# Where the normalised context rows are kept, and what ScalarE waits for before it writes them

## The chip, the cores and the metric

The kernel runs on one core of a Trainium2 chip. A core has five engines, each with its own queue of instructions in a fixed order: TensorE (PE in the profile; its weight loads are PEld), VectorE (DVE), ScalarE (ACT), GpSimd (POOL) and SyncE (SP, which starts the DMAs here). They meet only at semaphores. The metric is the time of one execution on the device in microseconds, median of the runs; lower is better.

## The reference

`x` is (128, 64, 128): 128 batch elements of 64 tokens and 128 features. `ctx_1024` (the context) has the same shape, `cond_1024` is (128, 128). Four layers follow each other:

```
L0: x += gate * selfattn(mod(ln(x)));  x += crossattn(ln(x), context);      x += gate * mlp(mod(ln(x)))
L1: x += crossattn(mod(ln(x)), mod(ln(context)))
L2: x += gate * selfattn(mod(ln(x)));  x += crossattn(ln(x), ln(context));  x += gate * mlp(mod(ln(x)))
L3: x += gate * mixture_of_3_experts(ln(x), evidence from context)
```

All attentions have 16 heads of 8 features. `ln` normalises the 128 features of a token. The context is normalised twice for each batch element, once in L1 and once in L2. The result of `ln(context)` depends on the input alone, and not on `x`.

## The kernel before

Work is cut into 32 groups of 4 batch elements (256 tokens). Six streams (`STREAMS`) each take every sixth group; a stream has its own set of tiles, and its next group starts when the one before is done. A group passes through `GROUP_STEPS`, some 75 steps such as `stats`, `normal`, `cols` (a layer norm and the transposition of its result), `q`, `k`, `v`, `tops`, `lows`, `scores`, `values`, `out` (an attention), `fc1`, `fc2` (an MLP). The order in which the steps of the six streams follow each other is a table, `SEQUENCE`, and it is the same on all engines: every engine walks `ORDER` from first to last and issues its own part of each step. So an instruction that waits holds up everything behind it on its engine, whatever stream that belongs to. In the middle of the table the pattern repeats: a stretch of some 343 us comes again and again.

PSUM has eight banks, in two halves of four. `tops` and `scores` take one half, and all other results of TensorE take the banks of the other half in turn. `bank_plan` fixes from the tables which bank each result takes, and who must have emptied it (`HELD_BEFORE`).

The steps that matter here, for a cross attention whose context is normalised:

- `stats` (VectorE, L1034 and L1037): mean and variance of the rows of `x`. In the same step ScalarE computes the normalised context rows, `cn_rows = c_rows * c_rstd + c_minus` (L1175, two instructions, one per half of 256 tokens). The scale and the offset were computed by GpSimd when the group began. This happens 64 times (32 groups, L1 and L2).
- `kvnorm` (TensorE, L802): `cn_rows` is transposed into PSUM, and ScalarE (L2) or VectorE (L1) moves it into `kvT`, from which keys and values are made.
- `normal` (VectorE, L1043) writes `n_rows`; `cols` (TensorE L802, then ScalarE L1163 or VectorE L1049 and L1050) turns them into `nT`, the normalised columns of x, for `q` or `fc1`.
- `lows`: TensorE turns the maxima of the scores (L870), and ScalarE moves them negated into `low` (L1163), a view of the tile `o_rows`. `scores` then uses `low` as a weight (L881), adds the scores (L885), and ScalarE takes the exponentials (L1212).
- `out` and `fc2`: VectorE adds the residual into `x_rows` (L1015 where it is gated, L1089 where not).

`cn_rows` is a view of the tile `o_rows`. That tile also holds `low` and, after `values`, the weighed rows that VectorE turns (L1079, L1082) before `out`. L1175 therefore waits, beside `c_scaled` (the scale is there), for `x_changed(n)`, that is, for the last residual sum of the same stream, which comes from the step `fc2` of L0 or from `out` of L2's self attention.

Of the kernel before, what the change touches and what calls it, by code (L numbers as in the profile page):

```python
# [257 lines left out]
def used_by(n, ring, back=0):  # L258

    s = ORDER[n][2]  # L260
    while back:
        n -= 1
        back -= ORDER[n][2] == s
    return int(USED[n][ring])


def residual_before(n):


    s, last, gated = ORDER[n][2], None, 0  # L270
    for m in range(n):
        kind, arg, t = ORDER[m]
        if t == s and kind == "load":
            last = None
        if t == s and kind in ("out", "fc2", "l3_out"):
            last = m
            gated += kind == "l3_out" or arg["gate"] is not None
    return last, gated


def round_of(n):

    return sum(kind == "load" and s == ORDER[n][2] for kind, _, s in ORDER[:n + 1]) - 1
# [80 lines left out]
def build(nc, x, cond, context, weights, biases, rows, ident_in, own_head_in, own_ones_in, gate_store, out):  # L364
# [3 lines left out]
    with ExitStack() as ctx:  # L368
# [3 lines left out]
        def each(name, shape, dt=F32):  # L372
            return [sb(f"{name}{i}", shape, dt) for i in range(STREAMS)]
# [23 lines left out]
        nT, kvT = each("nT", [D, GROUP, SEQ]), each("kvT", [D, GROUP, SEQ])  # L397
# [13 lines left out]
        o_rows = each("o_rows", [D, TOK])  # L411
        inv_sum = each("inv_sum", [D, GROUP * 4, 2])
        low = [o[:, 0:D] for o in o_rows]
        cn_rows = [o[:, :].rearrange("p (t c) -> p t c", t=2) for o in o_rows]
        weighed = [q[:, :, :, :].rearrange("p g l q -> p (g l q)") for q in q_heads]
        oT = kvT

# [107 lines left out]
        def x_changed(n):  # L525

            last, gated = residual_before(n)
            s = ORDER[n][2]
            if last is None:
                return x_in[s], 16 * (round_of(n) + 1)  # L530
            if ORDER[last][0] == "out" and ORDER[last][1]["gate"] is None:
                return v_emptied, used_by(last, FOR_VECTOR)
            return x_added[s], gated
# [12 lines left out]
        with nc.Block() as block:  # L546
# [37 lines left out]
            def _(pe):  # L584
# [7 lines left out]
                for n, (products, _) in enumerate(product_banks):  # L592
                    pe.wait_ge(turned_in, 3)
                    at = 0
                    for lhsT, rhs in products:
                        mm = nc.tensor.matmul(bank[7 if n == 0 else 3 + n][:, at:at + rhs.shape[1]], lhsT, rhs, start=True, stop=True)
                        at += rhs.shape[1]
                    mm.then_inc(products_filled, 1)
                pe.wait_ge(cond_moved, 2)
                for n in range(M_COND):  # L600
                    if n >= 4:
                        pe.wait_ge(mods_moved, n - 3)
                    dst = bank[n % 4][:, 0:B]
                    if n < M_EXPERT:
                        name, _, block_, _, _, _ = MODS[n]
                        mm = nc.tensor.matmul(dst, w(name, 0, block_), cond_silu[:, :], start=True, stop=True)
                    elif n < M_GATE:
                        e, r = divmod(n - M_EXPERT, 2)
                        mm = nc.tensor.matmul(dst, w("L3_e_w1", 3 * e + 2, 2 * 0 + r), mods[:, M_COND, :], start=True, stop=True)
                    else:  # L610
                        mm = nc.tensor.matmul(dst, w("L3_gate_w1", 2), mods[:, M_COND, :], start=True, stop=True)
                    mm.then_inc(mods_filled, 1)
# [10 lines left out]
                for n, (name, block_, _) in enumerate(GATES):  # L623
                    mm = nc.tensor.matmul(bank[6][0:B, n * D:(n + 1) * D], cond_silu[:, :], w(name, 0, block_), start=True, stop=True)
# [60 lines left out]
        with nc.Block() as block:  # L685
# [472 lines left out]
            def _(act):  # L1158
# [6 lines left out]
                for n, (kind, arg, s) in enumerate(ORDER):  # L1165
# [3 lines left out]
                    if kind == "stats" and n in CONTEXT_NORMS:  # L1169

                        e = CONTEXT_NORMS[n]
                        act.wait_ge(c_scaled[s], round_of(n) + 1)
                        act.wait_ge(*x_changed(n))
                        for t in range(2):
                            m = nc.scalar.activation(cn_rows[s][:, t, :], c_rows[s][:, t, :], ACT.Identity,  # L1175
                                                     scale=c_rstd[s][:, e, t:t + 1], bias=c_minus[s][:, e, t:t + 1])
                        m.then_inc(c_normed[s], 1)
# [123 lines left out]
```

## Time and profile before

| | us |
|---|---|
| median of 3 runs | 1933.61 (1929.34 to 1938.17) |
| time of the profiled execution | 1929.33 |
| its span, first to last instruction | 1927.5 |
| busy: PE, DVE, ACT, POOL | 1781.7, 1640.5, 1384.0, 643.6 |
| granted TensorE clock, mean share of full speed | 0.982 |

TensorE is busy for 92% of the span and VectorE for 85%. Matmul ends are modelled, so a busy TensorE isn't TensorE at its peak. The profiled execution took 1.8 us more than its span, and 4.3 us less than the median of the three runs. DMAs play no part after the start: the 16 DMA engines are busy below 10% from the third fortieth of the span on.

### The profile page before, as it was taken

Reading aid. Unit: us, or ns where it says so; the run is one execution under the profiler, and the core shown is the slowest. Engines: PE = TensorE matmul, PEld = TensorE weight load, DVE = VectorE, ACT = ScalarE, POOL = GpSimd, SP = SyncE. Lnnn points to the kernel's source line nnn. Section 1 sums busy time; section 2 is a strip of 40 time slices with the busy share of each in tenths; the row PEclk is TensorE's granted clock in tenths of the full one; section 3 lists DMA queues with packets and bytes.
Section 4 is the critical chain, followed back from the end, with each engine's and each line's share of the span. In section 5 each row is a group of like instructions: output and inputs, shape, how many; then the busy total and the mean of one; then the engine's idle time right before and its main releaser. Section 6 shows DMA issues by size and latency. Waiting matters only on the chain.

```text
span 1927.5 us, 88160 instructions
## 1 busy us (share of the span) xinstructions
PE 1781.7 (92%) x38181; PEld 1523.1 (79%) x38181; DVE 1640.5 (85%) x4236; ACT 1384.0 (72%) x3340; POOL 643.6 (33%) x1145
## 2 busy tenths in 40 slices
PE   3787999999999999999999999999999988989898
PEld 3666778888777888887878888787888877877788
DVE  2887889899988899997889999888999977988874
ACT  1554677787767778876777787777777776767697
POOL 1431324333323333442233333333333332332241
PEclk9999999999999999999999999999999999999999
DMA  4200000000000000000000000000000000000000
GB/s 164 61 13 9 17 17 14 17 22 22 22 22 9 16 23 22 22 23 22 3 22 22 23 22 22 22 3 22 22 22 23 22 9 18 20 14 9 9 5 15
DMA packets 57166, 42.62 MB, mean 22 GB/s; under 512 B 13520, under 2 KB 55632, under 8 KB 56528
## 3 DMA queue, kind: packets, MB, share of 16 engines
q1 hardware_dynamic: 56784, 36.99, 6.4%
q8 instruction: 306, 5.01, 1.0%
q14 instruction: 76, 0.62, 0.1%
HBM read 32.51 MB, written 4.46 MB: 19 GB/s over the span
## 4 chain that ended last, share of the span: by engine, by line
PE 66%; DVE 21%; ACT 7%; issue 3%; DMA 0%; POOL 0%; SPq 0%; ACTq 0%; DVEq 0%; POOLq 0%
PE half L981 9%; PE half L881 8%; PE half L861 7%; PE half L885 7%; PE half L900 6%; DVE top L1070 6%; PE half L928 4%; PE half L918 4%; PE half L802 4%; PE half L990 3%; PE half L848 3%; PE half L911 3%; PE half L837 3%; PE half L833 3%; ACT pT L1247 2%
## 5 line engine op out<-in xcount | busy, mean ns | idle before, releaser
L1070 DVE TENSOR_REDUCE top<-half 128x32 f32<-128x2048 f32 x160 | 365.0, 2282 | 63.0 <-PE half L861 61.9
L761 POOL TENSOR_TENSOR shifted<-moments,eps 128x2 f32<-128x2 f32 x256 | 50.6, 198 | 1091.0 <-DVE moments L1037 1090.9
L1212 ACT ACTIVATE pT<-half 128x512 f32<-128x512 f32 x640 | 327.9, 611 | 117.2 <-PE half L885 116.4
L881 PE MATMUL half<-o_rows,of_keys 32*128 32x128 f32 x5120 | 283.6, 290 | 16.3 <-ACT o_rows L1163 14.3
L885 PE MATMUL half<-q_heads,k_heads 32*128 32x128 f32 x5120 | 270.4, 279 | 1.6 <-issue 1.6
L881 PEld LDWEIGHTS half<-o_rows,of_keys 32*128 32x128 f32 x5120 | 214.9, 194 | 38.8 <-ACT o_rows L1163 20.3
L1247 ACT ACTIVATE pT<-half,mod 128x64 f32<-128x64 f32 x896 | 195.9, 334 | 48.5 <-PE half L981 47.3
L885 PEld LDWEIGHTS half<-q_heads,k_heads 32*128 32x128 f32 x5120 | 217.1, 196 | 2.8 <-issue 2.5
L861 PE MATMUL half<-k_heads,q_heads 32*128 32x128 f32 x5120 | 191.4, 285 | 9.9 <-issue 5.3
L1192 ACT ACTIVATE k_heads<-half,key_bias,own_head_sb 128x256 f32<-128x256 f32 x320 | 163.2, 570 | 46.3 <-PE half L837 45.0
L861 PEld LDWEIGHTS half<-k_heads,q_heads 32*128 32x128 f32 x5120 | 163.8, 191 | 37.7 <-issue 23.2
L1043 DVE TENSOR_SCALAR n_rows<-x_rows,moments,rstd 128x128 f32<-128x128 f32 x512 | 189.3, 416 | 3.9 <-POOL rstd L763 3.0
L763 POOL TENSOR_TENSOR rstd<-shifted,minus_halves 128x2 f32<-128x2 f32 x256 | 185.3, 724 | 20.1
L900 PEld LDWEIGHTS half<-pT,v_cols 128*32 128x32 f32 x10240 | 152.2, 110 | 38.1 <-issue 29.1
L900 PE MATMUL half<-pT,v_cols 128*32 128x64 f32 x10240 | 175.5, 220 | 6.7 <-ACT pT L1212 5.1
L1062 DVE TENSOR_SCALAR q_heads<-half,b_sb,own_head_sb 128x256 f32<-128x256 f32 x320 | 156.4, 532 | 11.9 <-PE half L833 11.7
L981 PE MATMUL half<-nT,w_sb 128*128 128x256 f32 x448 | 137.9, 390 | 0.0
L918 PE MATMUL half<-nT,w_sb 128*128 128x256 f32 x512 | 135.6, 393 | 1.0 <-DVE nT L1050 0.8
L1200 ACT ACTIVATE v_cols<-half 64x256 f32<-64x256 f32 x320 | 122.6, 383 | 18.6 <-PE half L848 16.5
L981 PE MATMUL half<-pT,w_sb 128*128 128x256 f32 x448 | 133.7, 380 | 0.0
L1217 ACT ACTIVATE pT<-half,b_sb 128x256 f32<-128x256 f32 x256 | 106.1, 471 | 35.6 <-PE half L918 34.4
L928 PE MATMUL half<-w_sb,pT 128*128 128x128 f32 x1024 | 127.3, 278 | 0.1
(151 smaller groups left out, 3747.3 us busy)
## 6 DMA issues: line engine op xcount, KB each, us to landing
gates<-gate_store SPq DMA_DIRECT2D x128, 128.0 KB, 3.0
x_rows<-x SPq DMA_DIRECT2D x32, 128.0 KB, 2.1
c_rows<-context SPq DMA_DIRECT2D x32, 128.0 KB, 2.7
out<-x_rows SPq DMA_DIRECT2D x32, 128.0 KB, 1.8
w_sb<-weights SPq DMA_DIRECT2D x1, 2368.0 KB, 12.7
pT<-weights SPq DMA_DIRECT2D x1, 1024.0 KB, 4.8
logit_bias<-logit_store SPq DMA_DIRECT2D x64, 1.5 KB, 3.5
row_sb<-rows SPq DMA_DIRECT2D x1, 769.5 KB, 6.3
```

The costliest lines, as they stand in the source:

```text
L763: nc.gpsimd.tensor_tensor(rstd[s][:, :], shifted[s][:, :], minus_halves[:, 0, :], ALU.pow).then_inc(rstd_in[s], 1)
L861: mm = nc.tensor.matmul(halves[HALF_OF[n]][:, g, tb * D:(tb + 1) * D], q_heads[s][part, tb, :, :], k_heads[s][part, tb, :, :], start=True, ...
L881: nc.tensor.matmul(halves[HALF_OF[n]][:, g, tb * D:(tb + 1) * D], of_keys[part, 2 * tb:2 * tb + 2, :], low[s][part, :], start=True, stop=F ...
L885: mm = nc.tensor.matmul(halves[HALF_OF[n]][:, g, tb * D:(tb + 1) * D], k_heads[s][part, tb, :, :], q_heads[s][part, tb, :, :], start=False ...
L900: mm = nc.tensor.matmul(dst[QUAD * g:QUAD * (g + 1), tb, :, lo, :], v_cols[s][:, at:at + QUAD], pT[s][:, g, tb, lo, :].rearrange("p (h q) ...
L918: mm = nc.tensor.matmul(dst[:, c * TOK:(c + 1) * TOK], w(layer["w1"], 0, 2 * half + c), nT[s][:, :, :], start=True, stop=True)
L928: mm = nc.tensor.matmul(dst[:, t * D:(t + 1) * D], hidden[s][:, c, t * D:(t + 1) * D], w(arg["w2"], c), start=c == 0, stop=c == 3)
L981: mm = nc.tensor.matmul(dst[:, r * TOK:(r + 1) * TOK], weight, src[:, :, :], start=c == 0, stop=c == 1)
L1043: m = nc.vector.tensor_scalar(n_rows[s][:, t, :], x_rows[s][:, t, :], moments[s][:, t, 0:1], rstd[s][:, t:t + 1], ALU.subtract, ALU.mult)
L1070: nc.vector.tensor_reduce(top[s][:, :].rearrange("p (g c) -> p g c", c=32)[:, :, 0:2 * GROUP], halves[HALF_OF[n]][:, :, :].rearrange("p g ...
L1212: nc.scalar.activation(turn_cols[s][:, g, :], halves[HALF_OF[n]][:, g, :], ACT.Exp, scale=ATT_SCALE).then_inc(scores_read, 1)
L1247: m = nc.scalar.activation(dst, src[:, at], ACT.Silu, bias=mod[s][:, k, tb:tb + 1])
```

## The change

The normalised context rows become a view of `nT` instead of one of `o_rows`, with the same shape (128 x 2 x 128), and ScalarE's wait for the residual sum is taken out. The rest of the program stands as it was.

```
-        cn_rows = [o[:, :].rearrange("p (t c) -> p t c", t=2) for o in o_rows]
+        cn_rows = [c[:, :, :].rearrange("p (t b) q -> p t (b q)", t=2) for c in nT]
...
                         e = CONTEXT_NORMS[n]
                         act.wait_ge(c_scaled[s], round_of(n) + 1)
-                        act.wait_ge(*x_changed(n))
                         for t in range(2):
                             m = nc.scalar.activation(cn_rows[s][:, t, :], c_rows[s][:, t, :], ACT.Identity,
                                                      scale=c_rstd[s][:, e, t:t + 1], bias=c_minus[s][:, e, t:t + 1])
```

After the first hunk `nT` has two uses: ScalarE writes the context rows into it at `stats`, TensorE reads them at `kvnorm`, and then `cols` of the same norm writes the columns of x over them. On ScalarE the line moves from L1175 to L1174, and those below it move up by one as well.

No instruction changes its place on any engine. This is the queue of ScalarE at one of the 64 places, in the stretch around 537 us of the trace, before:

```order
L1163 ACTIVATE o_rows2<-half0 128x128 [waits a_filled]
L1175 ACTIVATE o_rows1<-c_rows1,c_minus1,c_rstd1 128x128 [waits x_added1,c_scaled1]
L1175 ACTIVATE o_rows1<-c_rows1,c_minus1,c_rstd1 128x128
L1163 ACTIVATE kvT1<-half0 128x256 [waits a_filled]
L1163 ACTIVATE o_rows4<-half0 128x128 [waits a_filled]
L1212 ACT_TABLE_LOAD
L1212 ACTIVATE pT2<-half1 128x512 [waits scores_filled] x4
```

and of the change:

```order
L1163 ACTIVATE o_rows2<-half0 128x128 [waits a_filled]
L1174 ACTIVATE nT1<-c_rows1,c_minus1,c_rstd1 128x128 [waits c_scaled1]
L1174 ACTIVATE nT1<-c_rows1,c_minus1,c_rstd1 128x128
L1163 ACTIVATE kvT1<-half0 128x256 [waits a_filled]
L1163 ACTIVATE o_rows4<-half0 128x128 [waits a_filled]
L1211 ACT_TABLE_LOAD
L1211 ACTIVATE pT2<-half1 128x512 [waits scores_filled] x4
```

The number behind a tile is its stream. The output tile is another one and the semaphore `x_added1` is gone; the neighbours are the same.

## Rows read from the trace of the kernel before

**Rows 1.** The page: busy time by engine, and the shares of the chain.

```profile
PE 1781.7 (92%) x38181; PEld 1523.1 (79%) x38181; DVE 1640.5 (85%) x4236; ACT 1384.0 (72%) x3340; POOL 643.6 (33%) x1145
PE 66%; DVE 21%; ACT 7%; issue 3%; DMA 0%; POOL 0%; SPq 0%; ACTq 0%; DVEq 0%; POOLq 0%
```

**Rows 2.** L1175 alone: ScalarE's idle time before it; who waited for it (us, times).

```profile
  DVE x_rows L1015: 65.3, 31
  PE half L802: 27.0, 17
```

**Rows 3.** Timeline at 533 to 545 us: start, duration, engine, line, [idle before <-releaser].

```profile
532.91 0.28 ACT L1163 ACTIVATE o_rows<-half 128x128 f32<-128x128 f32 x1 [0.53 <-PE half L870]
...
534.49 0.61 PE L911 MATMUL half<-w_sb,kvT 128*128 128x128 f32 x4
...
537.30 0.88 ACT L1175 ACTIVATE o_rows<-c_rows,c_minus,c_rstd 128x128 f32<-128x128 f32 x2 [4.12 <-DVE x_rows L1015]
...
538.23 0.44 PE L802 MATMUL half<-ident_sb,o_rows 128*128 128x128 f32 x2 [3.13 <-ACT o_rows L1175]
...
544.60 0.43 DVE L1049 TENSOR_TENSOR half<-half,mod 128x256 f32<-128x256 f32 x1 [5.54 <-PE half L802]
```

**Rows 4.** Timeline two rounds of the pattern later, at 1223 to 1228 us.

```profile
1222.93 0.44 PE L802 MATMUL half<-ident_sb,o_rows 128*128 128x128 f32 x2 [3.13 <-ACT o_rows L1175]
...
1227.67 0.43 DVE L1049 TENSOR_TENSOR half<-half,mod 128x256 f32<-128x256 f32 x1 [3.92 <-PE half L802]
```

**Rows 5.** Timeline at 588 to 600 us.

```profile
588.27 1.57 ACT L1217 ACTIVATE pT<-half,b_sb 128x256 f32<-128x256 f32 x4
...
590.64 0.65 PE L848 MATMUL half<-w_sb,nT 128*32 128x64 f32 x32
...
593.08 0.88 ACT L1175 ACTIVATE o_rows<-c_rows,c_minus,c_rstd 128x128 f32<-128x128 f32 x2 [3.25 <-DVE x_rows L1015]
...
594.17 0.81 PE L881 MATMUL half<-o_rows,of_keys 32*128 32x128 f32 x8 [2.88 <-ACT o_rows L1163]
...
599.75 2.29 DVE L1070 TENSOR_REDUCE top<-half 128x32 f32<-128x2048 f32 x1 [5.96 <-PE half L861]
```

**Rows 6.** Timeline at 118 to 122 us: the same two instructions elsewhere.

```profile
118.76 0.50 PE L881 MATMUL half<-o_rows,of_keys 32*128 32x128 f32 x8 [0.37 <-ACT o_rows L1163]
...
121.93 2.29 DVE L1070 TENSOR_REDUCE top<-half 128x32 f32<-128x2048 f32 x1 [0.16 <-PE half L861]
```

**Rows 7.** Timeline at 244 to 258 us: VectorE's restart there.

```profile
256.14 2.29 DVE L1070 TENSOR_REDUCE top<-half 128x32 f32<-128x2048 f32 x1 [5.04 <-PE half L861]
```

**Rows 8.** Timeline at 154 to 165 us.

```profile
154.15 2.25 DVE L1070 TENSOR_REDUCE top<-half 128x32 f32<-128x2048 f32 x1
...
158.22 0.69 PE L802 MATMUL half<-ident_sb,o_rows 128*128 128x128 f32 x2 [3.23 <-ACT o_rows L1175]
...
164.93 2.29 DVE L1070 TENSOR_REDUCE top<-half 128x32 f32<-128x2048 f32 x1 [6.28 <-PE half L861]
```

**Rows 9.** Timeline at 1619 to 1622 us.

```profile
1619.00 0.44 PE L802 MATMUL half<-ident_sb,o_rows 128*128 128x128 f32 x2 [1.03 <-ACT o_rows L1175]
...
1621.33 1.19 PE L998 MATMUL half<-w_sb,pT 128*128 128x128 f32 x4 [1.89 <-ACT pT L1247]
```

**Rows 10.** Timeline at 282 to 285 us.

```profile
282.08 0.44 PE L802 MATMUL half<-ident_sb,o_rows 128*128 128x128 f32 x2 [1.14 <-ACT o_rows L1175]
...
284.27 2.29 DVE L1070 TENSOR_REDUCE top<-half 128x32 f32<-128x2048 f32 x1 [0.82 <-PE half L861]
```

**Rows 11.** Timeline, two more waits of TensorE for L1175.

```profile
109.00 0.44 PE L802 MATMUL half<-ident_sb,o_rows 128*128 128x128 f32 x2 [1.77 <-ACT o_rows L1175]
...
1708.31 0.44 PE L802 MATMUL half<-ident_sb,o_rows 128*128 128x128 f32 x2 [1.28 <-ACT o_rows L1175]
```

**Rows 12.** Windows: start:end, length, busy time of PE, PEld, DVE, ACT, POOL, PEclk, DMA share, GB/s.

```profile
538.71:542.13 3.42, 3.42 (x65) 3.42 (x68) 0.31 (x3) 1.83 (x3) 1.55 (x3) 0.53 0.02 5
...
908.00:910.00 2.00, 2.00 (x47) 2.00 (x42) 1.70 (x10) 0.21 (x1) 0.51 (x2) 0.50 0.63 179
```

More of the change, by code:

```diff
@@ L413, in build @@
         low = [o[:, 0:D] for o in o_rows]
-        cn_rows = [o[:, :].rearrange("p (t c) -> p t c", t=2) for o in o_rows]
+        cn_rows = [c[:, :, :].rearrange("p (t b) q -> p t (b q)", t=2) for c in nT]
         weighed = [q[:, :, :, :].rearrange("p g l q -> p (g l q)") for q in q_heads]
@@ L1172, in _ @@
                         act.wait_ge(c_scaled[s], round_of(n) + 1)
-                        act.wait_ge(*x_changed(n))
                         for t in range(2):
```

## The prediction, made before the change was run

> **What bounds the kernel now.** I began with the page. TensorE is busy for 92% of the span and VectorE for 85%, and the chain of work that ended last runs over TensorE for 66%, over VectorE for 21% and over ScalarE for 7% [rows 1]. So the pace is TensorE's, with stretches in which it waits for a result that came through VectorE, and ScalarE matters only where it is the messenger. ScalarE is such a messenger at the line that the change touches. The view of L1175 alone says that ScalarE stood idle before it for 65.3 us, in 31 of the 64 places, and that the last thing to come was always the residual sum of VectorE (L1015); TensorE in turn stood idle for 27.0 us, 17 times, because the context rows came late [rows 2]. All of TensorE's idle time is 1927.5 - 1781.7 = 145.8 us, so this one wait ends nearly a fifth of it. The other views are timelines around those places, read for two questions: when would ScalarE have been free, and what does VectorE wait for next. The second decides whether a gain lasts: every engine walks the same table, so a place gives its full gain when TensorE arrives earlier at a point where VectorE stood idle waiting for it for at least as long.
>
> **What the change costs.** Nothing is added. The two instructions at each place have the same input and the same shape, and write another tile of SBUF; I take 0.88 us per pair as before [rows 3]. A price of the other tile can't be read from the trace; since the same input and 128 output partitions are moved, I put it at nothing. The new home adds no wait: the last readers of `nT` before the place are TensorE's products for `fc1`, or for `q`, `k` and `v`, and ScalarE has itself already emptied the products, or taken the exponentials that depend on them. Behind it `cols` writes `nT` only after TensorE's transpositions, which come after `kvnorm` in its queue. The wait for the scale stays; GpSimd wrote it at the start of the group, tens of microseconds earlier.
>
> **What the removed wait gives, place by place.**
>
> *A, four places (the one at 537 us and its repetitions near 879, 1222 and 1565).* ScalarE is free at 532.91 + 0.28 = 533.19 and waits 4.12 us. TensorE ends `out` at 534.49 + 0.61 = 535.10 and waits 3.13 us for the rows [rows 3]. By the tables, the bank of this `kvnorm` was last held by a product of `fc1` that ScalarE has emptied, so VectorE doesn't hold it. Without the wait the rows are there at 533.19 + 0.88 = 534.07, and `kvnorm` starts at 535.10. From there to VectorE's restart (L1049) it took 544.60 - 538.23 = 6.37 us here, but 1227.67 - 1222.93 = 4.74 us two rounds later, over the same instructions [rows 3, 4]. The difference, 1.63 us, is TensorE's clock: it was granted 0.53 of full speed, that is the 1.2 GHz level nearly throughout, right after the gap at 538 [rows 12], and the full 2.4 GHz in the round at 1223. So VectorE restarts at 535.10 + 4.74 = 539.84 instead of 544.60: 4.76 us. VectorE is free from 544.60 - 5.54 = 539.06 on, so it doesn't stand in the way. Three of the four rounds are of this kind and one has no slow clock and gives 3.13 us: 3 x 4.76 + 3.13 = 17.4 us.
>
> *B, four places (near 250, 593, 937 and 1278).* TensorE doesn't wait for L1175 itself but for `low`, which stands behind it on ScalarE: 2.88 us at 594.17. ScalarE would be free at 588.27 + 1.57 = 589.84, done with the context rows at 590.72 and with `low` at about 591.0, and TensorE ends L848 at 590.64 + 0.65 = 591.29 [rows 5]. L881 starts then. From L881 to the restart of VectorE (L1070) it takes 121.93 - 118.76 = 3.17 us at full clock [rows 6], so VectorE restarts at 594.46 instead of 599.75: 5.29 us. It is free from 599.75 - 5.96 = 593.79 on. At the other three places VectorE's idle time is 0.92 us shorter, 5.04 instead of 5.96 (one stands in [rows 7]), since less of the way was at half clock; 5.29 - 0.92 = 4.4 us each. Sum 5.3 + 13.1 = 18.4 us.
>
> *157 us.* TensorE waits 3.23 us for L1175, but then needs the half of PSUM from which VectorE takes maxima until 154.15 + 2.25 = 156.40. `scores` starts at about 156.5, VectorE restarts at 159.7 instead of 164.93 [rows 6, 8]: 5.2 us.
>
> *1619 us.* TensorE waits 1.03 us for L1175 and 1.89 us for the expert activations behind it on ScalarE [rows 9]; with the slow clock that follows (1.63 as in A) 4.6 us.
>
> *C, four places (near 281, 625, 967, 1308).* TensorE waits 1.14 us, but VectorE idles only 0.82 us at its next wait for TensorE [rows 10]. I take 0.9 each: 3.6 us.
>
> *The rest.* At 109 us TensorE waits 1.77 us; at 1708 it is 1.28 us and a stretch at half clock follows, 2.9 with it [rows 11]. 1.8 + 2.9 = 4.7 us. Of the 27.0 us of [rows 2] these places hold 12.5 (A) + 3.2 + 1.0 + 4.6 (C) + 1.8 + 1.3 = 24.4. The other 2.6 us are small waits, mostly in a stretch that comes some 24 us behind C in each round, where VectorE works without a pause and TensorE stops for it again soon after; I put them at nothing, 2.6 us at most. What ScalarE waited beyond all this held up nobody that the trace shows.
>
> The sum is 17.4 + 18.4 + 5.2 + 4.6 + 3.6 + 4.7 = 53.9 us. Of it some 38 are idle time of TensorE and 16 are half clock (4.9 in A; 1.48 three times and 2.4 once in B; 1.2 to 1.7 at 157, 1619 and 1708).
>
> **The clock.** TensorE also fell to half speed where it had not stood still for long: at 908 to 910 us the granted clock is 0.50 [rows 12], and TensorE had gone from one product to the next before it with only short stops. There are three such stretches in the trace, none of which this wait explains, and each cost about what A shows, 1.63 us. So a part of the clock's 16 us may come back at other places. I allow for three new ones, 5 us, and forecast 53.9 - 5 = 49 us.
>
> The Trainium skill's page "TensorE: Matmul & The Clock Gate" has a rule for either side. Its section "HAM oscillation — how this bites in real kernels" says that a wait between bursts of matmuls lets the clock fall and the next burst starts slow; by that all 16 us come back and the gain is 54 us. The trace agrees at 538 and disagrees at 1223, where the same gap of 3.13 us was followed by full clock. The section "A second HAM failure mode: psum-queue depth-cycling" says that frequent small idle gaps between groups of matmuls are enough for the clock to swing, which speaks against counting the clock at all; the stretch at 908 agrees. That is the second rival below.
>
> The profiled execution took 1929.33 us; less 49 is 1880. The median of the runs shown lies 4.3 us higher, so the forecast is **1884 us**, 2.6% below 1933.61.
>
> **The rivals.**
>
> *VectorE takes the pace* (chance 0.17). It is busy for 85% of the span and in the steady part for more. What TensorE gains at the places above is drawn from idle time that VectorE then no longer has, and if other waits of TensorE for VectorE grow in return, only part stays. Against it: at each large place VectorE's own idle time is longer than the gain. Half of the gain would stay: 1933.6 - 27 = 1906 us.
>
> *The clock doesn't come back* (0.14). TensorE falls to half speed as often as before, at other gaps. For it: the three stretches without a long gap. Only the 38 us of idle time are won: 1896 us.
>
> *It doesn't do what it says* (0.06). The context rows are early, but TensorE finds the next obstacle at the same place, a bank that VectorE has still to empty, or the maxima that it has still to take, as at 157 [rows 8]. Against it: at A the bank is ScalarE's, and at B L881 was held by `low`, which only ScalarE had still to write [rows 5]. Then the gain is what is left at 109 and C, some 0 to 5 us: 1931 us.
>
> *Slower* (0.03). TensorE, now stopping in many small steps and not in a few long ones, drops to half clock more often. A stretch costs 1.63 us. With all 53.9 - 16 = 38 us of idle time won, it takes more than 23 new stretches before the kernel is slower, against 13 or so now; with 30 of them it is 1945 us. Only if the idle time is not won either does a handful suffice.
>
> **How the numbers follow.** The forecast has 0.60, and its own range is 1872 (all of the sum, 54 us, and 8 us for what I put at nothing: the 2.6 us above, and places where ScalarE waited and something other than L1175 was late in consequence) to 1896. The range for 8 in 10 reaches up to most of the first rival: 1868 to 1908. What a measurement of this kernel can tell from no change is about 0.5%, 9.7 us. The forecast and the first two rivals are faster by more, and a sliver of the third: 0.92. Same: 0.05. Slower: 0.03.
>
> **What would show it.** In the profile of the changed kernel the line of the context rows (L1174) has no idle time that VectorE's residual sum ends, and no wait of TensorE for it above 0.5 us. VectorE's idle time of 5.54 and 5.96 us at the restarts of A and B [rows 3, 5] falls below 1 us. TensorE's busy time falls too, by about as much as the half clock gives back, and the mean granted clock rises from 0.982 to about 0.99. The repeating stretch shrinks from 343 us to about 333. The prediction is wrong if the gaps of 3 us at A and B are still there under another releaser, or gone while the repeating stretch keeps its length; and the sum is wrong in its clock term if the idle time goes but the granted clock stays at 0.98.

## The result, and the profile after

| kernel | median us | lowest to highest | runs |
|---|---|---|---|
| before | 1931.47 | 1928.68 to 1938.17 | 4 |
| after | 1868.8 | 1866.06 to 1869.83 | 4 |

The changed kernel takes 0.9668 of the time, with a 95% interval of 0.9639 to 0.9698: some 63 us less, where 49 were forecast. The profiled execution took 1866.06 us, its span is 1864.3 us and its mean granted clock 0.996. The time lies 15 us under the forecast of 1884. That is 3 us below the low end of the forecast's own range (1872), and just inside the range for 8 in 10 (1868 to 1908).

Lines of the page of the changed kernel: busy time by engine, TensorE's granted clock in 40 slices of the span, the chain that ended last, and VectorE's maxima (busy us, mean ns, idle time ahead of them). The last line is the same row before.

```profile
PE 1756.0 (94%) x38181; PEld 1502.5 (81%) x38181; DVE 1639.4 (88%) x4236; ACT 1383.1 (74%) x3340; POOL 643.9 (35%) x1145
...
PEclk9899999999999999999999999999999999999999
...
PE 74%; DVE 14%; ACT 6%; issue 3%; DMA 0%; POOL 0%; SPq 0%; DVEq 0%; POOLq 0%
...
L1070 DVE TENSOR_REDUCE top<-half 128x32 f32<-128x2048 f32 x160 | 365.1, 2282 | 29.4 <-PE half L861 27.8
...
L1070 DVE TENSOR_REDUCE top<-half 128x32 f32<-128x2048 f32 x160 | 365.0, 2282 | 63.0 <-PE half L861 61.9
```

Against [rows 1] the number of matmuls is unchanged and TensorE is busy for 25.7 us less; its idle time is 1864.3 - 1756.0 = 108.3 us, where it was 145.8. That is 37.5 us less idle time and 25.7 us less busy time for the same work, together the 63.2 us by which the span is shorter. VectorE's share of the chain fell from 21% to 14%. It is busy for as long as before and only waits less: ahead of its maxima 29.4 us, where it was 63.0.

The view of the line of the context rows in the changed kernel (durations in ns, then who idled before it and who for it):

```profile
L1174 ACT ACTIVATE nT<-c_rows,c_minus,c_rstd x128: 478/487/554, 105.8 to 1774.7; 128x128 f32<-128x128 f32 x128
its engine sat idle before it (us, times) until:
who waited for it (us, times):
  PEld half L802: 0.2, 1
```

Both numbers of [rows 2] are gone: nothing stands under "sat idle before it", where there were 65.3 us, and TensorE's 27.0 us have shrunk to a single 0.2 us.

The timeline of the changed kernel at the first of the four places A, which answers to [rows 3]:

```profile
519.80 0.28 ACT L1163 ACTIVATE o_rows<-half 128x128 f32<-128x128 f32 x1 [0.52 <-PE half L870]
519.98 0.87 ACT L1174 ACTIVATE nT<-c_rows,c_minus,c_rstd 128x128 f32<-128x128 f32 x2
...
521.39 0.61 PE L911 MATMUL half<-w_sb,kvT 128*128 128x128 f32 x4
...
521.84 0.38 PE L802 MATMUL half<-ident_sb,nT 128*128 128x128 f32 x2
...
526.51 0.43 DVE L1049 TENSOR_TENSOR half<-half,mod 128x256 f32<-128x256 f32 x1 [0.57 <-PE half L802]
```

ScalarE goes from the copy straight to the context rows, TensorE goes from `out` straight to `kvnorm`, and VectorE waits 0.57 us where it waited 5.54. From `kvnorm` to VectorE's restart it is 526.51 - 521.84 = 4.67 us; I had reckoned with the 4.74 of [rows 4].

The same at the second of the four places B, which answers to [rows 5]:

```profile
570.17 1.57 ACT L1216 ACTIVATE pT<-half,b_sb 128x256 f32<-128x256 f32 x4
...
571.61 0.89 ACT L1174 ACTIVATE nT<-c_rows,c_minus,c_rstd 128x128 f32<-128x128 f32 x2
...
572.54 0.65 PE L848 MATMUL half<-w_sb,nT 128*32 128x64 f32 x32
...
573.12 0.50 PE L881 MATMUL half<-o_rows,of_keys 32*128 32x128 f32 x8
...
576.15 2.29 DVE L1070 TENSOR_REDUCE top<-half 128x32 f32<-128x2048 f32 x1 [0.44 <-PE half L861]
```

L881 has no idle time before it any more (2.88 us before), and VectorE waits 0.44 us (5.96 before). Windows of five microseconds around the place A show full clock (the columns are those of [rows 12]):

```profile
520.00:525.00 5.00, 5.00 (x117) 4.83 (x120) 4.90 (x13) 3.34 (x8) 1.20 (x2) 1.00 0.02 5
525.00:530.00 5.00, 5.00 (x210) 4.43 (x207) 4.15 (x16) 4.99 (x12) 1.74 (x4) 1.00 0.02 5
```

**Where the 63 us came from, place by place.** VectorE takes its maxima (L1070) 160 times, in the same order in both kernels. If the start of each is subtracted from the start of its counterpart before, the difference is a staircase, and each step is what one place gave:

| place (time in the kernel before) | forecast | step measured |
|---|---|---|
| 109 us | 1.8 | 2.0 |
| 157 us | 5.2 | 5.4 |
| A, four places | 17.4 | 4.97, 4.44, 3.34, 4.98: 17.7 |
| B, four places | 18.4 | 4.57, 5.52, 4.05, 4.39: 18.5 |
| C, four places | 3.6 | 0.87, 1.19, 1.19, 1.37: 4.6 |
| 1619 us | 4.6 | 5.46 and 1.36: 6.8 |
| 1708 us | 2.9 | 3.5 |
| the small waits some 24 us behind C, four places | 0 | 0.91 each: 3.6 |
| stretches at half clock near 225, 908 and 1248 us | -5 (the old three stay, three new ones) | 2.15, 1.63, 1.63: 5.4, the old ones gone |
| all other steps, up and down, 1.8 at most | 0 | -4.2 |
| sum | 48.9 | 63.3 |

### The profile page after: what moved, and what is told of

Its sections match the earlier page's. It is cut to its first block, busy times and chain, and to the rows that moved or that the text cites. A ratio compares the mean times of both kernels' runs of the same rounds, so it can differ in the third digit from the quotient of the medians.

```text
span 1864.3 us, 88096 instructions
## 1 busy us (share of the span) xinstructions
PE 1756.0 (94%) x38181; PEld 1502.5 (81%) x38181; DVE 1639.4 (88%) x4236; ACT 1383.1 (74%) x3340; POOL 643.9 (35%) x1145
## 4 chain that ended last, share of the span: by engine, by line
PE 74%; DVE 14%; ACT 6%; issue 3%; DMA 0%; POOL 0%; SPq 0%; DVEq 0%; POOLq 0%
PE half L981 9%; PE half L881 8%; PE half L861 7%; PE half L900 7%; PE half L885 7%; PE half L928 5%; PE half L918 5%; DVE top L1070 4%; PE half L802 4%; PE half L990 4%; PE half L848 4%; PE half L911 3%; PE half L833 3%; PE half L837 3%; ACT pT L1246 2%
## 5 line engine op out<-in xcount | busy, mean ns | idle before, releaser
L1070 DVE TENSOR_REDUCE top<-half 128x32 f32<-128x2048 f32 x160 | 365.1, 2282 | 29.4 <-PE half L861 27.8
L881 PE MATMUL half<-o_rows,of_keys 32*128 32x128 f32 x5120 | 273.8, 281 | 5.1 <-ACT o_rows L1163 3.0
L885 PE MATMUL half<-q_heads,k_heads 32*128 32x128 f32 x5120 | 261.4, 271 | 3.0 <-issue 2.9
L881 PEld LDWEIGHTS half<-o_rows,of_keys 32*128 32x128 f32 x5120 | 205.9, 186 | 26.3 <-issue 11.5
L885 PEld LDWEIGHTS half<-q_heads,k_heads 32*128 32x128 f32 x5120 | 207.8, 187 | 5.4 <-issue 5.4
L861 PEld LDWEIGHTS half<-k_heads,q_heads 32*128 32x128 f32 x5120 | 160.0, 186 | 37.3 <-issue 21.6
L1062 DVE TENSOR_SCALAR q_heads<-half,b_sb,own_head_sb 128x256 f32<-128x256 f32 x320 | 156.6, 533 | 10.4 <-PE half L833 10.0
## 6 DMA issues: line engine op xcount, KB each, us to landing
w_sb<-weights SPq DMA_DIRECT2D x1, 2368.0 KB, 12.7
```

What stands on the lines that cost most here:

```text
L861: mm = nc.tensor.matmul(halves[HALF_OF[n]][:, g, tb * D:(tb + 1) * D], q_heads[s][part, tb, :, :], k_heads[s][part, tb, :, :], start=True, ...
L881: nc.tensor.matmul(halves[HALF_OF[n]][:, g, tb * D:(tb + 1) * D], of_keys[part, 2 * tb:2 * tb + 2, :], low[s][part, :], start=True, stop=F ...
L885: mm = nc.tensor.matmul(halves[HALF_OF[n]][:, g, tb * D:(tb + 1) * D], k_heads[s][part, tb, :, :], q_heads[s][part, tb, :, :], start=False ...
L1070: nc.vector.tensor_reduce(top[s][:, :].rearrange("p (g c) -> p g c", c=32)[:, :, 0:2 * GROUP], halves[HALF_OF[n]][:, :, :].rearrange("p g ...
```

## The experiments

**Home only: the new tile with the old wait.** Does the tile matter, or only the wait?

```
                         e = CONTEXT_NORMS[n]
                         act.wait_ge(c_scaled[s], round_of(n) + 1)
+                        act.wait_ge(*x_changed(n))      # the rest as in the changed kernel
```

> The context rows live in nT as in the change, but ScalarE's wait for the residual sum is put back. Theory (the wait is everything): ratio to the kernel before 1.000 within 0.3%, 65 us of idle time before the line again. Rival (the other tile itself saves or costs something): a ratio away from 1 by more than 0.3%, up to the whole 0.967.

Measured: 1932.28 us (1925.04 to 1942.49, 10 runs), ratio 1.0 (0.998 to 1.002) to the kernel before. The view of its line, with the wait back:

```profile
L1175 ACT ACTIVATE nT<-c_rows,c_minus,c_rstd x128: 477/492/553, 109.5 to 1838.8; 128x128 f32<-128x128 f32 x128
its engine sat idle before it (us, times) until:
  DVE x_rows L1015: 65.2, 31
...
  PE half L802: 26.8, 17
```

The rows land in `nT` and everything is as before: 65.2 us in 31 places, 26.8 us in 17. The new home costs nothing and gives nothing; all of the gain is the wait's.

**One kind of norm keeps the wait.** Half of the 64 context norms, those of the kind LOOSE (all of them in L1), keep it; then the other half, of the kind TIGHT (all in L2).

```
+                        if CONTEXT_NORMS[n] == LOOSE:   # the other run: == TIGHT
+                            act.wait_ge(*x_changed(n))
```

> The change, with the wait kept for the 32 context norms of L1 (whose residual sum comes from fc2) and gone for the 32 of L2. By place: A, B, 157 and 1619 us belong to L2, so 17 + 18 + 5 + 5 = 46 us of the 54 of the sum are won, plus what the clock gives beyond it: about 1876 to 1882. Rival (the gain is spread over all waits of ScalarE, in proportion to its idle time): about half of 63 us, 1900.

> The mirror image: the wait gone for L1 and kept for L2. By place only C, 109 and 1708 us are won, 3.6 + 4.7 = 8 us: 1923. Rival (spread): 1900.

Measured: with LOOSE waiting 1877.08 us (1874.20 to 1879.79), ratio 0.9719 (0.9694 to 0.9745); with TIGHT waiting 1919.5 us (1916.68 to 1925.49), ratio 0.9942 (0.9919 to 0.9965). Against the 1931.84 us of the kernel before in the same set of runs, 54.8 us are won without the wait of the TIGHT norms, to which all places A and B belong, and 12.3 us without that of the LOOSE ones. The first time lies in the range expected (1876 to 1882), though 9 us more were won than the 46 of the places; the second is 3.5 us under the 1923 expected. The two gains sum to 67, not to 63, so the split holds to a few microseconds.

**The wait placed behind the rows.** Is it enough to have the rows early, or must the wait go?

```
-                        act.wait_ge(*x_changed(n))      # ahead of the two activations
                         ... (the two activations)
+                        act.wait_ge(*x_changed(n))      # behind them
```

> The change, with the wait for the residual sum put behind the two instructions instead of in front of them. The context rows are then early, but what stands behind them on ScalarE is as late as before. Theory (A and C are rows that come late, B and 1619 are the queue behind them): A, C, 109 and 157 stay won, B and 1619 are lost, 23 us and their clock: about 1892 to 1900. Rival (it is the queue behind the line that matters everywhere): nearly the time of before, 1925 or more. Rival (only the rows matter): 1870.

Measured: 1903.59 us (1899.50 to 1904.83), ratio 0.985 (0.9821 to 0.9878). Only 28 of the 63 us are won, fewer than the 32 to 40 expected. The timeline of this kernel at the place B shows why:

```profile
582.71 0.89 ACT L1174 ACTIVATE nT<-c_rows,c_minus,c_rstd 128x128 f32<-128x128 f32 x2
...
586.00 0.28 ACT L1163 ACTIVATE o_rows<-half 128x128 f32<-128x128 f32 x1 [2.40 <-DVE x_rows L1015]
...
586.33 0.50 PE L881 MATMUL half<-o_rows,of_keys 32*128 32x128 f32 x8 [2.04 <-ACT o_rows L1163]
...
590.69 2.29 DVE L1070 TENSOR_REDUCE top<-half 128x32 f32<-128x2048 f32 x1 [3.92 <-PE half L861]
```

The rows themselves are early, but ScalarE now stands at the wait with the copy for `low` behind it, and TensorE needs that copy: 2.04 us of its 2.88 are back. At A the copy of the transposed rows (into `kvT`) stands behind the wait in the same way. Both are in this kernel's list of waits (total us, times, longest):

```profile
ACT kvT L1163 <- DVE x_rows L1015: 16.7, 5, 3.5
...
ACT o_rows L1163 <- DVE x_rows L1015: 12.5, 5, 2.6
```

The expectation was wrong on this point: it had A and 157 us as wholly won. Measured as in the table above (starts of the maxima, here against the changed kernel), this kernel loses 1.6 to 1.7 us at each place A and 4.6 us at 157, beside 2.1, 3.5, 1.6 and 1.9 at B. The wait's price is not only in what it guards but in all that is queued behind it.

**The wait kept at the four places A, or at the four places B.** What is one gap worth, clock included?

```
+                        if n in (738, 1284, 1830, 2376):    # A; the other run: (276, 822, 1368, 1914), B
+                            act.wait_ge(*x_changed(n))
```

> The change, with the wait put back at the four places A alone (context norms of L2 near 537, 879, 1222 and 1565 us). Theory (the places add up and the clock falls because of these gaps): 4 x 3.13 = 12.5 us of idle time come back and half clock of 1.6 to 1.8 us behind most of them: 17 to 20 us above the change, 1886 to 1889. Rival (the clock falls by chance, wherever TensorE is at the time, and stays away in a faster kernel): 12.5 us, 1881.

> The change, with the wait put back at the four places B alone (near 250, 593, 937 and 1278 us). Theory: 4 x 2.9 = 11.6 us of idle time and 1.5 to 2.4 us of half clock behind each: 18 to 20 us above the change, 1887 to 1889. Rival (clock by chance): 1880.

Measured: A 1891.62 us (1889.67 to 1894.49), ratio 0.9801 (0.9776 to 0.9826), that is 22.8 us over the changed kernel; B 1884.57 us (1878.38 to 1888.69), ratio 0.9758 (0.9722 to 0.9794), 15.8 us over it. The timeline of the kernel with the wait at A, first place:

```profile
524.99 0.69 PE L802 MATMUL half<-ident_sb,nT 128*128 128x128 f32 x2 [3.13 <-ACT nT L1176]
...
532.44 0.43 DVE L1049 TENSOR_TENSOR half<-half,mod 128x256 f32<-128x256 f32 x1 [6.64 <-PE half L802]
```

and its windows around that place:

```profile
520.00:525.00 5.00, 1.86 (x18) 1.68 (x16) 4.86 (x14) 0.88 (x2) 1.20 (x2) 0.90 0.00 2
525.00:530.00 5.00, 5.00 (x79) 4.67 (x83) 0.77 (x6) 2.20 (x4) 1.74 (x4) 0.50 0.01 3
530.00:535.00 5.00, 5.00 (x196) 4.55 (x192) 2.38 (x8) 4.64 (x11) 0.00 (x0) 0.92 0.01 2
```

The idle time of 3.13 us is that of [rows 3] to the hundredth, but the way to VectorE's restart is 532.44 - 524.99 = 7.45 us, where the kernel before had 6.37 with one stretch at half clock and 4.74 with none. The clock of 0.90, 0.50 and 0.92 in three windows of 5 us takes 0.5 + 2.5 + 0.4 = 3.4 us, two stretches of 1.7 in a row. Behind all four gaps of this kernel the clock fell, twice for 3.4 and twice for 1.7 us. So the wait at A cost more than the 17 to 20 us expected and the one at B less than the 18 to 20; behind the four gaps of B the clock fell twice only. Times of different sets of runs carry some uncertainty of their own: the median of the kernel before was 1929.8 us beside these two and 1931.5 to 1932.0 beside the others, so 22.8 and 15.8 may be 2 to 3 us too low.

**The gaps kept, and filled.** This is the run that separates idle time from clock in the kernel before: TensorE still waits for the rows, but multiplies meanwhile. Six products of the identity with a weight tile go into the PSUM slot that the next transposition overwrites.

```
                     if kind == "kvnorm":
+                        slot = (to_v if isinstance(arg[1], tuple) else to_a).slot()
+                        if n in (151, 739, 1285, 1831, 2377):
+                            keep_busy(slot)             # 6 matmuls, results overwritten
                         count.next(c_normed[s])
...
                     if kind == "scores":
+                        wait_emptied(pe, HELD_BEFORE[n], emptied)
+                        if n in (279, 825, 1371, 1917):
+                            keep_busy(halves[HALF_OF[n]][:, 0, :])
                         after("low", s)
-                        wait_emptied(pe, HELD_BEFORE[n], emptied)
```

The products stand behind the wait for the slot and ahead of the wait for the data; for that the order of the two waits is turned round at every `kvnorm` and every `scores`. The trace records each product as two instructions, so six are 12.

> The kernel before, with the wait where it was, but at the four places A, the four places B and at 157 us TensorE fills its gap with six products (identity by weights, 2.6 us) whose result is overwritten. They change no output. Theory (the gaps make the clock fall): the idle time stays on the path, the half clock goes: 9 places at 1.5 to 2.4 us, 13 to 16 us faster than before, 1916 to 1919. Rival (the clock falls for another reason than standing still): no change, 1932, or slower where the fillers run over the end of a gap.

Measured: 1913.82 us (1910.61 to 1914.65), ratio 0.9912 (0.9887 to 0.9937), 16 us less than the kernel before, with more work and the same waits. The timeline and one window of this kernel at the first place A:

```profile
530.07 0.44 PE L802 MATMUL half<-ident_sb,o_rows 128*128 128x128 f32 x2 [0.54 <-ACT o_rows L1184]
...
534.81 0.43 DVE L1058 TENSOR_TENSOR half<-half,mod 128x256 f32<-128x256 f32 x1 [3.92 <-PE half L802]
```

```profile
530.00:535.00 5.00, 4.93 (x137) 4.64 (x138) 1.05 (x7) 4.22 (x9) 1.74 (x4) 1.00 0.02 5
```

534.81 - 530.07 = 4.74 us and clock 1.00: exactly the way of [rows 4]. In this profile the clock fell behind none of the nine filled gaps, where it had fallen behind eight of the nine before. Only what TensorE does while it waits was changed, so the 16 us are its clock. Not all of them need come from the nine places: the old stretches near 228, 908 and 1248 are gone as well, and a new one stands near 558.

**The gaps A kept and filled, in the changed kernel.** The same edit on the kernel that keeps the wait at A, n in (739, 1285, 1831, 2377), without the part for `scores`.

> The change, with the wait put back at the four places A, and six products (identity by weights, 2.6 us, overwritten afterwards, no output changes) in front of the context rows' transposition there. The version without the products took 1891.6 us, 22.8 more than the change. Theory (a gap of 3.13 us costs itself and the half clock that follows): 12.5 us stay, the rest goes: 1881. Rival (A costs more than its gap because something else is late there, not the clock): 1889 or more.

Measured: 1881.06 us (1880.43 to 1881.83), ratio 0.9739 (0.972 to 0.9759). Its timeline, first place A:

```profile
521.82 2.75 PE L807 MATMUL half<-w_sb,ident_sb 128*128 128x256 f32 x12
...
525.12 0.44 PE L802 MATMUL half<-ident_sb,nT 128*128 128x128 f32 x2 [0.54 <-ACT nT L1183]
...
529.85 0.43 DVE L1056 TENSOR_TENSOR half<-half,mod 128x256 f32<-128x256 f32 x1 [3.92 <-PE half L802]
```

TensorE is busy for 2.75 us of the gap, stops for 0.54, and the way behind it is 4.73 us instead of 7.45. Of the 22.8 us that the four gaps A cost, 10.5 were clock (1891.62 - 1881.06) and 12.3 are the wait itself, 3.1 each: the 3.13 us of the rows, four times. The two times are of different sets of runs; each against its own kernel before, the clock's part is 12.7 us. In the profiles the places A of this kernel lose 3.4 us three times and 4.5 once against the changed kernel, so the split is good to some 2 us and not to a tenth.

**The change once more, and with a busy start.** The second adds eight products while TensorE waits for the first DMAs, so that its clock is up when the work begins.

```
+                keep_busy(bank[7], 4)                   # ahead of the loop over ORDER
...
                     if kind == "cols":
+                        if n == FIRST_COLS:
+                            keep_busy(bank[7], 4)
```

> The change itself, again. Its time is 1867 to 1870. Asked is how much time the clock takes from it from run to run: the kernel before had mean clocks of 0.978 to 0.986 in its runs. If unexplained falls of the clock are chance and about as many as before (three to six a run), the mean clock lies at 0.990 to 0.993; if they go with the gaps, at 0.995 or above (0.996 is what is lost in the first 60 us alone).

> The change, with eight products (identity by weights, into a bank that isn't in use; no output changes) while TensorE waits for the first rows: four before the first transposition and four before the second. From 44 to 59 us the clock is at half in the change, and the work done in it is some 5 us. Theory: with TensorE kept busy, the clock is full when that work begins, and 2 to 3 us are saved: 1866. Rival (the wait for the rows hides the slow clock, or the products delay the first steps): 1869 or more. The difference is at the edge of what can be told.

Measured, on one chip: the change 1868.3 us (1867.05 to 1872.89), ratio 0.9678 (0.9656 to 0.9699); with the busy start 1863.46 us (1860.65 to 1866.51), ratio 0.9648 (0.9627 to 0.967). The windows of the start, first the changed kernel:

```profile
54.00:56.00 2.00, 1.54 (x4) 1.27 (x5) 1.23 (x5) 0.00 (x0) 1.50 (x3) 0.50 0.41 128
56.00:58.00 2.00, 2.00 (x37) 1.30 (x36) 1.54 (x6) 1.29 (x3) 1.69 (x4) 0.50 0.56 70
```

and the one with the busy start:

```profile
54.00:56.00 2.00, 1.98 (x40) 1.40 (x39) 1.72 (x6) 1.08 (x3) 0.84 (x4) 1.00 0.36 108
56.00:58.00 2.00, 2.00 (x38) 1.69 (x36) 1.76 (x6) 0.86 (x3) 1.84 (x4) 1.00 0.65 101
```

The same first products run at the 2.4 GHz level (clock 1.00) instead of the 1.2 GHz level (0.50), and the median is 4.8 us lower. This version beats both kernels. But the start does not account for the 4.8 us. In the two profiles VectorE's first maxima begin 2.3 us earlier with the busy start (57.32 against 59.59 us), as expected, and by 78 us the lead is gone (78.26 against 77.97), for with the busy start the clock fell at 69 us. The 4.4 us between the two spans build up later; the largest steps, 3.6 and 3.3 us, are where the profile of the repeated change has two stretches at half clock (222 and 502 us) and this one has none. That the products of the start prevent those is not shown.

The repeated change answers its own question. Its four executions had mean clocks of 0.994, 0.994, 0.992 and 0.990. One lies within what I had put down for falls by chance, as many as before (0.990 to 0.993), one at its low end, two just above it, and none at the 0.995 or above that falls by the removed gaps alone would give. So the changed kernel still loses its clock now and then. These windows of the profiled one,

```profile
220.00:225.00 5.00, 3.34 (x34) 2.84 (x34) 3.27 (x5) 0.93 (x4) 0.00 (x0) 0.73 0.02 3
...
500.00:505.00 5.00, 3.48 (x23) 2.61 (x19) 4.93 (x8) 1.29 (x4) 2.36 (x3) 0.72 0.01 2
```

stand against these of the first profile of the same kernel:

```profile
220.00:225.00 5.00, 3.91 (x68) 3.26 (x58) 4.33 (x8) 1.78 (x7) 0.00 (x0) 1.00 0.02 3
...
500.00:505.00 5.00, 3.85 (x50) 3.24 (x52) 4.90 (x12) 2.86 (x12) 1.39 (x3) 1.00 0.01 3
```

The same program keeps full clock at 220 and 500 us in one execution and loses it in another. A single profile can't tell whether such a stretch belongs to a kernel. What stood ahead of the fall differed too. At 221.7 us TensorE's stop was longer in the repeated run (first line) than in the first profile (second line), and nothing in the profile shows what ended it ("issue"):

```profile
221.66 1.52 PE L861 MATMUL half<-k_heads,q_heads 32*128 32x128 f32 x29 [1.79 <-issue]
...
221.84 1.16 PE L861 MATMUL half<-k_heads,q_heads 32*128 32x128 f32 x29 [1.09 <-issue]
```

Near 500 us it was 1.52 against 0.97 us.

## Why the prediction was right in its mechanism and 14 us short

**Right: what bounds the kernel, and that the wait was false cost.** No line waits for the residual sum at the context rows any more, VectorE's idle time at A and B is 0.57 and 0.44 us (I had said below 1), and the repeating stretch shrank from 342 to 330 us (333 forecast; both from VectorE's restart at C to the next). The new home costs nothing, which the run with the home alone shows at a ratio of 1.0.

**Right: the large terms.** A, B and 157 us were forecast at 17.4, 18.4 and 5.2 us and measured at 17.7, 18.5 and 5.4. They came from one rule: the new start is the time at which the second-last thing is ready, and the way from there to VectorE's restart is read where the same instructions ran at full clock [rows 4, 6]. The idle term as a whole, 38 us, was measured at 37.5. That it is so close is in part luck: it holds 4.6 us of waits that I had put too low (see below) and 4.2 us of small steps back that I hadn't foreseen.

**Wrong: the clock term.** I forecast 16 us from half clock less an allowance of 5 for new stretches, 11 net. TensorE's busy time fell by 25.7 us over the same instructions. Two steps of it failed. In the table they make 10.4 and 2.2 of the 14.4 us between sum and measurement; the small waits below make 3.6 and 1.0, the other places together 1.4, and 4.2 go off again.

- The allowance. "I allow for three new ones, 5 us": I took the three stretches without a long gap in front of them (one is in [rows 12]), left them in place, and added three more. In the changed kernel's profile there is no such stretch in the loop at all; the old three gave back 5.4 us. That is 10.4 of the 14.4 us. The half of it that the old three gave back was luck of the one profile. The repeated profile shows two stretches at a mean clock of 0.994, the first one none at 0.996, so one costs 0.001; the eight executions of the change had 0.990 to 0.996, 0.993 in the mean, which by this estimate is about three stretches each, as many as the three of before. What failed is the three new ones, 5 us: I had no row that spoke for them, and on the average they didn't come.
- The price of one place. I put one stretch of 1.63 us at 1619 us; the granted clock there was at half for 6.8 us, which costs 3.4, two stretches in a row, and the step was 6.8 instead of 4.6. A whole stretch costs about 1.7 us, and a place can have two.

**Wrong: the small waits that I put at nothing.** The four waits some 24 us behind C gave 0.91 each, 3.6 us, over my bound of 2.6, and the places C gave 1.0 more than I took. I had argued that VectorE works without a pause there. It does, but its next wait for TensorE, 5 to 6 us later, shrank from 1.0 to 0.1 us. What VectorE does at the moment is not decisive if it is going to wait for TensorE a few microseconds later. The stops of TensorE that the removed wait had ended there were 0.5 to 0.6 us; why 0.9 came of them is open. The 4.2 us of small steps back are the most that the rival "VectorE takes the pace" can claim; what ended each of them I have not traced.

**The rivals.** "The clock doesn't come back" is refuted from two sides: the busy time fell, and with the gaps merely filled 16 us come back in the kernel before. "It doesn't do what it says" and "slower" have nothing left. Of the two rules of the Trainium skill's page "TensorE: Matmul & The Clock Gate" that I weighed, the one in the section "HAM oscillation — how this bites in real kernels" is borne out: with the gaps A filled, and the rows arriving just as late, 10.5 us come back. The other, "A second HAM failure mode: psum-queue depth-cycling", would as I read it have left the clock as low as before. Behind its first 60 us TensorE still stops 128 times in the changed kernel, for 63 us together and never for over 2; in the kernel before there were 137 stops of that size, for 74 us. They hardly changed in number, and the mean clock went from 0.982 to 0.996 (0.990 to 0.996 over eight executions). Of the falls that are left, this says nothing.

**Still open.** Why the clock falls near 220 and 500 us in some executions and not in others. Of the twelve profiles seven have a fall at 219 to 229 us and four at 500 to 510 us. All but one of these eleven (219 us, in the run with the wait behind the rows) stand behind or at a stop of TensorE of 1.5 to 2.0 us, and in the profiles without a fall there that stop was 1.5 us at most. So its length, which changes from one execution to the next, is the suspect. It is no more than that: elsewhere a stop of 1.63 us passed without a fall (1539 us in the kernel before), what makes the stop long I don't know, and no run here varied it on purpose. The two old stretches near 908 and 1248 us stand some 27 us behind a place A and have no such stop ahead of them; near 228 there was one, of 1.64 us. The profiles of kernels with the gaps A gone have no stretch like those two, which may or may not be chance.

## What to carry to other kernels

- In an engine that works its queue in order, a wait costs what it guards and all that stands behind it. Ask whether it guards a value or only a tile that is shared, and whether another tile is free at that time; putting it two instructions later recovered only 28 of 63 us.
- To price a gap of TensorE, take the gap and the slow stretch behind it: here four gaps of 3.13 us cost 12.3 + 10.5 us. Do not allow for new stretches, beyond those that the trace already has, without a row that shows what would make them.
- Where a gap can't be removed, products into a PSUM slot that is about to be overwritten keep the clock: 16 us in the kernel before, and 10.5 us in the changed kernel with the gaps A.

## What the runs showed of the hardware that I had not expected

- After a gap of 3.13 us the granted clock fell in 15 of 16 cases (the four places A in the profiles of the kernel before, home only, TIGHT waiting, and the wait at A), after one of 2.84 to 2.94 us in 11 of 16 (the four places B in the first three of these and the wait at B). Behind the 13 gaps that were filled (nine in one run, four in the other) it fell in none. Of two rounds of the same program with the same gap one can have the fall and the other not, so it has to be counted as a share and not as yes or no. One fall took 1.7 us, and some came as two in a row, 3.4 us.
- The spread of the kernel's own time goes mostly with the clock: of 33 runs of the kernel before, the six fastest took 1925.0 to 1925.8 us at mean clocks of 0.983 to 0.988, thirteen took 1932.0 to 1935.0 at 0.979 to 0.985, and the two slowest 1939.2 and 1942.7 at 0.978. The changed kernel with the gaps A kept had 1889.7 to 1894.5 us at 0.986 to 0.989; with them filled, 1880.4 to 1881.8 at 0.993 to 0.994.
- Products that nobody reads, and that take TensorE some 2.75 us at a place, made a kernel faster by 16 us of 1930.
